# Moving the second chunk's two normalisations six rounds later in a hand-ordered graph-network kernel

## The reference

```python
x = _layernorm(x + _L0_gnn_ref(x, adj, ...), axis=-1)
x = _layernorm(x + _L1_gnn_ref(x, adj, ...), axis=-1)
x = _layernorm(x + _L2_gnn_ref(x, adj, ...), axis=-1)
x = _layernorm(x + _L3_gnn_ref(x, adj, ...), axis=-1)

# L0: Chebyshev terms I, A, 2A@A-I applied to x, then a weight of its own for each node
w = einsum('nd,dkio->nkio', embedding, weight)      # 16 numbers d per node
out = einsum('bnki,nkio->bno', x_g, w) + b
# L1: attention, kept only where adj > 0.5; on these inputs it comes to elu(mean over the nodes)
# L2: (A + I) @ (x W' + b) / degree
# L3: three steps v = relu([v, A v] W1' + b1) W2' + b2
```

## Time and profile before

| what | value |
|---|---|
| runs | 1033.38, 1032.51, 1032.59 us; median 1032.59 |
| the profiled execution | 1033.26 us, of which the span is 1031.5 us |
| PE busy | 1008.9 us, 98% |
| DVE, ACT, POOL busy | 678.2 us (66%), 456.5 us (44%), 555.2 us (54%) |
| mean granted TensorE clock | 0.996 |
| chain that ended last | PE 83%, DVE 9%, ACT 3%, DMA 2%, issue 1% |

### The profile page before, as it was taken

How to read it: one execution, slowest core, us unless ns; L and a number is a source line. 1 busy time by engine, 2 the same in 40 slices (tenths; PEclk the granted TensorE clock), 3 DMA queues, 4 the chain that set the end, 5 groups by cost and what they waited for, 6 DMA issues and landing times.

```text
span 1031.5 us, 18649 instructions
## 1 busy us (share of the span) xinstructions
PE 1008.9 (98%) x6854; PEld 485.1 (47%) x6854; DVE 678.2 (66%) x1683; ACT 456.5 (44%) x1109; POOL 555.2 (54%) x645
## 2 busy tenths in 40 slices
PE   7999999999999999999999999999999999999995
PEld 3445444444444444434445556555555545455552
DVE  3886565656577796577667767786763546657556
ACT  4632233453345545543552554342556555232632
POOL 0004498666558698879878465474534243323311
PEclk9999999999999999999999999999999999999998
DMA  9930000000000000000010111000032231000022
GB/s 367 403 141 1 1 2 2 1 2 1 1 1 2 1 2 2 1 2 1 1 42 1 41 42 42 2 1 1 2 123 98 107 123 42 3 2 21 21 62 62
DMA packets 14658, 45.65 MB, mean 44 GB/s; under 512 B 960, under 2 KB 9280, under 8 KB 10080
## 3 DMA queue, kind: packets, MB, share of 16 engines
q1 hardware_dynamic: 14560, 44.39, 11.8%
HBM read 40.19 MB, written 4.19 MB: 43 GB/s over the span
## 4 chain that ended last, share of the span: by engine, by line
PE 83%; DVE 9%; ACT 3%; DMA 2%; issue 1%; POOL 0%; SPq 0%; ACTq 0%; DVEq 0%; POOLq 0%
PE PS L961 28%; PE PS L924 23%; PE PS L794 21%; DMA BW<-at_in 2%; PE PS L779 2%; PE PS L781 2%; PE PS L780 2%; DVE BW L1227 1%; DVE T L1230 1%; ACT WZ L1074 1%; DVE X L1230 1%; DVE X L1542 1%; PE PS L788 1%; PE PS L787 1%; PE PS L786 1%
## 5 line engine op out<-in xcount | busy, mean ns | idle before, releaser
L794 PE MATMUL PS<-BW,S 128*128 128x512 fp8e4 x1280 | 290.9, 379 | 1.2 <-DVE R L1230 0.7
L1074 ACT ACTIVATE T<-PS,SM 128x128 f32<-128x128 f32 x384 | 113.1, 366 | 208.5 <-DVE X L1230 127.3
L924 PE MATMUL PS<-WZ,R 64*128 64x512 f16 x1536 | 198.0, 377 | 1.7 <-ACT T L1074 1.7
L794 PEld LDWEIGHTS PS<-BW,S 128*128 128x128 f16 x1280 | 120.2, 98 | 150.1 <-issue 17.0
L961 PE MATMUL PS<-BW,S 128*128 128x512 fp8e4 x768 | 173.1, 379 | 0.0
L1748 POOL TENSOR_TENSOR T<-T 128x128 f32<-128x128 f32 (+1 forms) x192 | 125.0, 651 | 73.0 <-ACT T L1074 62.9
L1230 DVE SCALAR_TENSOR_TENSOR X<-PS,SM,X 128x128 f32<-128x128 f32 x320 | 109.6, 342 | 77.8 <-PE PS L924 76.9
L924 PEld LDWEIGHTS PS<-WZ,R 64*128 64x128 f16 x1536 | 69.5, 94 | 104.6 <-issue 26.3
L961 PEld LDWEIGHTS PS<-BW,S 128*128 128x128 f16 x768 | 73.8, 98 | 83.3 <-issue 0.5
L961 PE MATMUL PS<-BW,T 128*128 128x512 fp8e4 x480 | 109.3, 379 | 0.0
L1748 POOL TENSOR_TENSOR S<-R,S 128x512 f16<-128x512 f32 (+1 forms) x46 | 52.7, 1153 | 102.4 <-ACT S L1074 102.4
(11 more groups left out here) (210 smaller groups left out, 1494.6 us busy)
## 6 DMA issues: line engine op xcount, KB each, us to landing
WZ<-a_in SPq DMA_DIRECT2D x16, 1024.0 KB, 4.8
BW<-at_in SPq DMA_DIRECT2D x8, 1024.0 KB, 19.1
R<-at_in SPq DMA_DIRECT2D x7, 1024.0 KB, 13.8
out<-X SPq DMA_DIRECT2D x16, 256.0 KB, 2.3
X<-x_in SPq DMA_DIRECT2D x3, 1024.0 KB, 21.1
T<-w_in SPq DMA_DIRECT2D x1, 1536.0 KB, 16.6
R<-at_in SPq DMA_DIRECT2D x2, 512.0 KB, 4.5
SM<-sm_in SPq DMA_DIRECT2D x1, 520.5 KB, 19.2
```

The costliest lines, as they stand in the source:

```text
L794: m = e.matmul(o, stile(h, t, c), Bm[:, t, block(j)], start=(t == 0 and h == 0), stop=(last and t == NT - 1 and h == 1))
L924: m = e.matmul(bank(b0 + q), halves[kd][zh][r, :], WZ[r, wh, kd, block(g)], start=(i == 0), stop=(i == 8))
L1074: return e.activation(o, i, f, **kw)
```

## The change

One line of `middle_order` becomes conditional. `g` is from there on the round from which the steps of chunk c after layer 0's `red` are counted, so for chunk 1 all of them stand six rounds later: var(0,1) in 41, rs and apply(0,1) in 42 to 45, sum in 45, mean and row_a in 47, row_b in 48, addrow in 49 to 52, sq(1,1) in 51 to 54, red in 52 to 55, var(1,1) in 55, rs, apply and split (1,1) in 56 to 59. Within one round chunk 1's steps stand before chunk 2's and before the round's `bt`. The squares and sums of layer 0 (the lines above) stay, and so do chunks 0, 2 and 3, all `bt`, `chk`, `E2`, `dx`, `t1` and all of `TAIL`. No instruction is added or removed.

```diff
             at(g + 4 * j + (4 if late else 6), ("sq", 0, c, j))
             at(g + 4 * j + (4 if late else 7), ("red", 0, c, j))
-        g += 16
+
+        g += 22 if c == 1 else 16
         if c < 3:
             at(g + 3, ("var", 0, c))
             at(g + 4, ("rs", 0, c), ("apply", 0, c, 0))
```

## The result

The changed kernel takes 1036.97 us (median of 6 runs, 1036.05 to 1037.26) where the kernel before takes 1032.99 (6 runs; it was 1032.59 in the three that the forecast started from): a ratio of 1.0039, interval 1.0029 to 1.0049. It is 4.0 us slower; the forecast was 1.3 us slower, with a range that ended at 1035.6. The profiled execution has a span of 1035.2 us against 1031.5.

A forecast was written before the change was run, and what follows sets the result against it. PE, busy 98% of the span, was taken as the bound, so only its waits count: 2.0 us won and 3.3 lost through POOL's queue give +1.3, a median of 1033.9 us from 1032.59, range 1030.5 to 1035.6.

The forecast's parts named there:

- The waits at 369 and 454: PE's waits in round 37 (1.32 us) and for bank 0 before E2 of round 51 (0.71): both end, 2.0 us won.
- the 0.3 of rs(1,0): The remaining 0.3 us of PE's wait at L832, the first matmul of a `t1`, said to stay.
- the sum: Whole kernel: 2.0 us won and 3.3 lost give +1.3 us, within -0.8 and +3.0.
- The chain of adds: POOL without pause from add(55), rounds 56 to 59: add(60) begins at 516.2 before DVE's slowing, against 509.8 in a calm course.
- 3.3: PE's new wait through POOL's queue, 1.2 us plus 2.1 for DVE's slowing of POOL, between 1.2 and 5.0.
- the 1.96 us from an add to PE's second half two rounds on: PE's second half of round g+2 begins no sooner than 1.96 us after add(g), read from round 0.
- DVE's share: Rounds 56 to 59: apply, rs and row_b on DVE slow POOL by 2.1 us in all, between none and 3.8.
- full lock: Rule against the change: each apply costs POOL its whole 0.67, four times 0.33 more, sum +2.6; 0.34 was kept.
- The tail begins with POOL some 4 us late: Tail: POOL's lateness priced at nothing, up to 0.5 us, as POOL waits for chunk 3's applies and PE has other products.
- E2 of round 59: Before round 60: 1.1 us of spare meets an apply of 0.7 to 1.4, up to 0.3 lost, within the 3.3.
- Rival A: Rounds 56 to 59: POOL pays more, each like round 52 with 0.94, PE's wait 5.0, 1035.6 us; chance with part of another 0.22.
- new waits in the tail: Listed among the signs that the forecast is wrong, without a size.

The follow-up runs named there:

- e3: Changed kernel with the bt of rounds 60, 61 and 62 put into 50, 51 and 53: 1034.83 us, ratio 1.0016 to the kernel before.
- e1: Changed kernel with the five bt of rounds 56 to 59 put into 50 to 53: 1031.81 us, ratio 0.9988 to the kernel before.
- e2: Kernel before, chunk 1's norms in their old place, five bt of rounds 40 to 48 put into 60, 61 and 62: 1035.83 us, ratio 1.0029.
- e7: Changed kernel, bt of 56 to 59 in 50 to 53, of 60 to 62 in 42 to 44, `rows` at tail position 11, not 8: 1034.83 us, ratio 1.0019.
- e9: Changed kernel with `rows` moved from tail position 8 to the end of round 63: 1035.05 us, ratio 1.0021 to the kernel before.
- e6: Changed kernel with `rows` moved from position 8 of the tail to 11: 1038.22 us, ratio 1.0052 to the kernel before.

## Why the prediction was wrong

**Right: what is won.** The waits at 369 and 454 are gone. Rounds 37 and 51 take 6.27 and 5.82 us where they took 7.66 and 6.60, 2.2 us in all; the 0.3 of rs(1,0) stayed. With 3.6 lost in rounds 60 to 62 the middle came out at +1.4, where the sum had +1.3.

**Right, in part by luck: POOL's queue and its price in the middle.** The chain of adds, 31.4 us for four rounds, came out to 0.1 us, and the 1.96 us from an add to PE's second half two rounds on held exactly for the adds of rounds 59 and 60 (behind that of 58, whose three instructions took 0.5 longer, it was 2.5). PE lost 3.6 us where 3.3 was forecast, in rounds 60, 61 and 62 where 61 or 62 was said.

DVE's share was 2.1 as taken, though spread otherwise (rounds of 8.66, 7.54, 7.23 and 7.93, where 8.8, 7.1, 7.25 and 8.3 were said). That it met the total was luck. Beside the four applies POOL's instructions grew by 0.55, 0.33, 0.85 and 0.51, 2.2 us together where four times 0.34 was taken, and beside rs and row_b, priced at 0.6 and 0.16, no growth is to be seen. Taken as a full lock that costs POOL each apply whole (0.67), as I had read the rule in the Trainium skill, "SBUF — State Buffer", section "Who interferes with whom", the four rounds would have been 1.3 us longer, which they were not. But an apply cost 0.56 in the mean, so its price was nearer to that reading than to mine. Which engine pays depends on how the two meet: the apply at 488.48 was held itself, the one at 494.56 was not, and the POOL instruction beside it took 1.29 where the same one takes 0.45 alone. DVE and POOL at both:

```profile
488.48 1.19 DVE L1543 TENSOR_TENSOR X<-X,T 128x512 f32<-128x512 f32 x1
487.96 1.15 POOL L1749 TENSOR_TENSOR S<-X,S 128x512 f16<-128x512 f32 x1
489.19 1.60 POOL L1749 TENSOR_TENSOR X<-X,bc 128x512 f32<-128x512 f32 x1
...
494.56 0.68 DVE L1543 TENSOR_TENSOR X<-X,T 128x512 f32<-128x512 f32 x1
494.47 1.29 POOL L1749 TENSOR_TENSOR T<-T 128x128 f32<-128x128 f32 x1
```

**Wrong: "The tail begins with POOL some 4 us late ... and I price it at nothing, up to 0.5 if that cover is thin."** The lateness was right (3.6 us). The tail cost 3.0 us: from Z of round 63 to the end are 513.3 us where they were 510.3. The reasons given were that POOL waits there for chunk 3's applies anyway and that PE has other products. The first is the mistake: POOL's idle 3.7 us before sum(3) are the same length in both kernels, because those applies themselves hang on the late add. The kernel before, then the changed one:

```profile
535.74 1.65 POOL L1748 TENSOR_TENSOR SM<-X 128x512 f32<-128x512 f32 x1 [3.71 <-DVE X L1542]
...
540.04 1.65 POOL L1749 TENSOR_TENSOR SM<-X 128x512 f32<-128x512 f32 x1 [3.73 <-DVE X L1543]
```

POOL's idle time is no cover when what it waits for has been started by POOL itself. The second holds for 78 us only, until PE needs W and D, and there the kernel before was already waiting, 0.87 us at 608.46. A chain at whose end PE waits has little slack, whatever its engines' busy shares are: 3.6 us late made `W(2,1)` 2.8 later after Z of round 63 (87.30 to 90.09 us), 0.5 late (e3) made it 0.5 later, and 0.95 late (e1) only 0.2. Why e1 lost less than e3 is open. e2 shows the price by itself, e3 the middle nearly without it, and e1 that chunk 1's later place adds no more than the 0.7 in front of round 60. That the delay passes through chunk 3's norm on DVE and ACT is read from the traces, and e7 and e9, where `rows` moves within that chain, agree with it.

**Small, and near.** E2 of round 59 was priced at up to 0.3 and was 0.7 in e1 and 1.1 in e3. The changed kernel's profile has no such wait, but e6 and e9, which are the same as it up to round 62, have 1.1 and 0.9 there and 2.1 and 2.0 in round 62: the middle's loss is spread otherwise from one execution to the next, and is 3.0 to 3.6 us in all. Rival A (slower, POOL pays more) had the right sign and the wrong place: its extra 1.7 us were looked for in rounds 56 to 59. The range ended where the middle's bounds did, since no rival held a price for the tail, though "new waits in the tail" stood among the signs of being wrong.

## What to carry to other kernels

When a step moves, add up the queue of each in-order engine in its new place, with the filler work that a schedule put into the old gap: here the bt's gap stayed at 50 to 53 while the splits left it, and moving five of them turned 4 us lost into 1 us won. A late engine is paid twice if it also starts a chain that something needs later: follow its last late instruction forward to the next wait of the bounding engine, and take any wait found there in the old profile as a sign that the chain has little slack. Idle time of an engine covers a delay only if what ends that idle time does not come from the delayed work itself.

## What the runs showed of the hardware that was not expected

**A small DVE instruction can be as long as a large one.** The step `rows` took 6.2 us in the kernel before, 6.7 in e7 and 4.5 in e9 (529.56 to 534.06), for nine instructions of at most 128 columns, and POOL was busy in all three. What differs is where they fall. The one of 16 columns began at 563.85 in e7 beside a POOL add that had begun at 563.61, and took 1.06 us, until 0.03 after that add's end. In e9 it began 0.08 us before POOL's next instruction, and took 0.17:

```profile
563.61 1.27 POOL L1752 TENSOR_TENSOR X<-X,ROW 128x512 f32<-128x512 f32 x1
...
529.64 1.27 POOL L1749 TENSOR_TENSOR X<-X,ROW 128x512 f32<-128x512 f32 x1
```

In the kernel before, 29 TENSOR_SCALAR instructions of DVE with 2 to 128 columns and no PSUM operand took over 0.5 us. 28 of them began beside a running POOL instruction, and each ended 0.02 to 0.09 us after it (not every one that began so was long). Those of one column in `rows` took 0.15 to 0.21 us even there.

**A large apply and POOL hold each other up.** In the same trace the applies that began well after the start of a POOL instruction ended 0.55 to 0.58 us after its end, and grew from 0.67 to as much as 1.77. POOL's next instruction, where it followed within 0.08 us, grew by 0.33 to 0.36 (from 0.45 to 0.78 at 128 columns, from 1.27 to 1.60 at 512), which fits the 0.34 that the prediction read from the earlier trace rows. Where an apply began within 0.04 us of a POOL instruction, as at 485.28 and 500.37 in the changed kernel, it kept its 0.69 and POOL's instruction grew by 0.5.
